# Three of a block's turns by DMA instead of TensorE, and another list of the round, in a four-layer graph network on one Trainium2 core

## The reference

```python
# 0: GCN over the normalized adjacency, two linear layers (256-512-256), each with a batchnorm over all tokens
x = _layernorm(x + _L0_gnn_ref(x, adj, ...))
# 1: Chebyshev mix, linear, layernorm, relu, plus x (x1); masked attention with 4 heads, plus x1, layernorm (x2);
#    MLP 256-512-256 with gelu, plus x2, layernorm
x = _layernorm(x + _L1_gnn_ref(x, adj, adj, ...))
# 2: two graph convolutions, then for p = 1..4 an LSTM over windows of p tokens whose last state replaces a token
x = _layernorm(x + _L2_gnn_ref(x, adj, ...))
# 3: Wh = x @ W; attention from s1 + s2, leaky relu, mask, softmax; attention @ Wh
x = _layernorm(x + _L3_gnn_ref(x, adj, ...))
```

## Time and profile before

| | us |
|---|---|
| median of 3 runs | 2158.94 |
| lowest, highest | 2158.62, 2160.29 |
| the profiled execution, its own time | 2162.29 |
| its span, first to last instruction | 2160.5 |
| TensorE busy in the span | 2017.1 |
| VectorE busy | 1749.8 |
| ScalarE busy | 1451.9 |

### The profile page before, as it was taken

One profiled execution on the slowest core, in us unless ns is written; L12 is line 12 of the kernel. 1 busy time (PEld: TensorE's weight loads), 2 busy tenths in 40 slices (PEclk: granted clock), 3 DMA queues, 4 the chain that ended last, 5 costly groups with the idle time before them and its releaser, 6 DMA issues. The chain is left out here.

```text
span 2160.5 us, 86772 instructions
## 1 busy us (share of the span) xinstructions
PE 2017.1 (93%) x37609; PEld 1780.4 (82%) x37609; DVE 1749.8 (81%) x4987; ACT 1451.9 (67%) x4411; POOL 187.0 (9%) x259
## 2 busy tenths in 40 slices
PE   6979769999999999999999999999999999999986
PEld 3434358989898989889898989898989998899985
DVE  6779767888888888888888888888888888888865
ACT  5657336767776777667676776676767766676775
POOL 2000000000001000100010000101010001000000
PEclk9989789999999999999999999999999999999998
DMA  7847300000100001000100010000000010000000
GB/s 277 289 173 267 107 11 12 13 12 3 41 3 22 3 3 42 12 12 3 42 13 12 3 41 13 12 3 28 16 22 3 3 42 12 12 3 12 3 12 12
DMA packets 36825, 87.85 MB, mean 41 GB/s; under 512 B 2416, under 2 KB 26992, under 8 KB 32752
## 3 DMA queue, kind: packets, MB, share of 16 engines
q1 hardware_dynamic: 36464, 82.56, 11.0%
HBM read 52.15 MB, written 30.41 MB: 38 GB/s over the span
## 5 line engine op out<-in xcount | busy, mean ns | idle before, releaser
L1443 ACT ACTIVATE pool_mem<-ps,lstm_b 128x64 f32<-128x64 f32 (+2 forms) x2496 | 603.9, 354 | 191.8 <-PE ps L252 186.4
L250 PE MATMUL ps<-hl_a,w_hi 128*128 128x64 f16 (+2 forms) x3776 | 545.6, 215 | 31.9 <-DVE hl_a L623 16.0
L251 PE MATMUL ps<-hl_a,w_hi 128*128 128x64 f16 (+2 forms) x3776 | 544.3, 215 | 0.0
L252 PE MATMUL ps<-hl_a,w_lo 128*128 128x64 f16 (+2 forms) x3776 | 543.8, 215 | 0.0
L250 PEld LDWEIGHTS ps<-hl_a,w_hi 128*128 128x128 f16 x3776 | 350.5, 98 | 64.0 <-DVE hl_a L623 17.1
L251 PEld LDWEIGHTS ps<-hl_a,w_hi 128*128 128x128 f16 x3776 | 350.2, 98 | 24.4 <-issue 3.0
L252 PEld LDWEIGHTS ps<-hl_a,w_lo 128*128 128x128 f16 x3776 | 350.2, 98 | 24.4 <-issue 3.0
L250 PE MATMUL ps<-hl_b,w_hi 128*128 128x84 f16 (+2 forms) x2112 | 366.3, 228 | 2.5 <-ACT pool_mem L1443 1.7
L251 PE MATMUL ps<-hl_b,w_hi 128*128 128x84 f16 (+2 forms) x2112 | 366.0, 228 | 0.0
L252 PE MATMUL ps<-hl_b,w_lo 128*128 128x84 f16 (+2 forms) x2112 | 364.3, 228 | 0.0
L250 PE MATMUL ps<-pool_mem,w_hi 128*128 128x64 f16 (+2 forms) x3072 | 352.4, 200 | 2.2 <-DVE pool_mem L1716 2.0
(11 more groups left out here) (244 smaller groups left out, 4402.1 us busy)
## 6 DMA issues: line engine op xcount, KB each, us to landing
xa<-in_x SPq DMA_DIRECT2D x32, 512.0 KB, 5.5
h_scratch<-pool_mem SPq DMA_DIRECT2D x14, 1024.0 KB, 4.3
pool_mem<-h_scratch SPq DMA_DIRECT2D x14, 1024.0 KB, 6.8
pool_mem<-in_wpack SPq DMA_DIRECT2D x16, 704.0 KB, 4.3
out<-xb SPq DMA_DIRECT2D x16, 512.0 KB, 3.4
o_scratch<-act_in SPq DMA_DIRECT2D x14, 512.0 KB, 3.2
act_in<-o_scratch SPq DMA_DIRECT2D x14, 512.0 KB, 5.4
row<-in_rows SPq DMA_DIRECT2D x1, 1408.0 KB, 11.4
```

Of the source, the lines that this page charges most:

```text
L250: nc.tensor.matmul(o, l[0], r[0], start=first, stop=False, skip_group_check=True)
L251: nc.tensor.matmul(o, l[0], r[1], start=False, stop=False, skip_group_check=True)
L252: return nc.tensor.matmul(o, l[1], r[0], start=False, stop=last, skip_group_check=True)
L1443: op = nc.scalar.activation(gates[s][h][:, g, m * w:(m + 1) * w], gate_place(s, h, g, m, w), ACT.Tanh, bias=lstm_b[:, bias:bias + 1], scal ...
```

## The change

The three turns leave TensorE. ScalarE and VectorE split x1, x2 or xc while it still lies by token, into `by_token_hl` (in the place of the LSTM's state, which is free then): ScalarE's `turn_high` writes hi from the buffer x1, VectorE's `turn_low` writes x1 minus hi. SP then issues two transposing DMAs per half, each from 128 tokens x (2 parts x 256 features) to 4 blocks of 128 features x 128 tokens in hl_b, and v, mlp_up and gat wait until both have landed. In diff form, cut:

```diff
+            TURNS = ["x1", "x2", "xc"]
+            turn_hi = Signal("turn_hi", " ".join(TURNS))
+            turn_lo = Signal("turn_lo", " ".join(TURNS))
+            turned = Signal("turned", " ".join(TURNS))
...
+                def landed(self, s, n, h, which):
+
+                    sem, count = self.at(s, n, h, which)
+                    return sem, count * HALF * 16
...
+                def turn(s, n, h, which):
+                    sp.wait_ge(*turn_lo.at(s, n, h, which))
+                    for b in range(HALF):
+                        a = h * HTOK + b * P
+                        sp.dma_start(hl_b[s][:, :, :, a:a + P].rearrange("p c k n -> p (c k) n"),
+                                     by_token_hl[s][h][:, b, :, :].rearrange("p c d -> p (c d)"), transpose=True)\
+                            .then_inc(turned.of(s, h), 16)
...
-                def turn(s, n, h, src, which):
-
-                    bank = FEAT_BANK[which][h]
-                    for f in range(KT):
-                        for b in range(HALF):
-                            mm = nc.tensor.transpose(fea(s, bank)[:, f, b * P:(b + 1) * P],
-                                                     src[s][:, h * HALF + b, f * P:(f + 1) * P], ident[:, :])
-                    mm.then_inc(feat_ps.of(s, h), 1)
...
                 def value(s, n, h):
-                    pe.wait_ge(*feat_lo.at(s, n, h, "x1"))
+                    pe.wait_ge(*turned.landed(s, n, h, "x1"))
...
+                    nc.scalar.copy(by_token_hl[s][h][:, :, 0, :], x1[s][:, blocks(h), :]).then_inc(turn_hi.of(s, h), 1)
...
+                def turn_low(s, n, h, which):
+                    dve.wait_ge(*turn_hi.at(s, n, h, which))
+                    hi, lo = (by_token_hl[s][h][:, :, c, :] for c in range(2))
+                    nc.vector.tensor_tensor(lo, x1[s][:, blocks(h), :], hi, ALU.subtract).then_inc(turn_lo.of(s, h), 1)
```

```diff
+                    if (base, s, n) not in reached:
+                        reached.add((base, s, n))
+                    elif base == "turn_x1" and n > 1:
+                        store_tile(s, n - 1)
+                    elif base == "turn_x2" and n < ROUNDS:
+                        load_next_o(s, n)
+                    elif base == "hid3" and n < ROUNDS:
+                        load_next_x(s, n)
```

The list ROUND has the same steps in another order (two of its lines, the first of each):

```diff
-1:xa_bias.0 1:turn_x1.0 0:inp3.0 0+norm_y 1:cheb.1 0:hid3.1 0:cell3.0 0:pack3.1 1:conv.1 0:hid3.0 1:norm_g1.1
+1:cheb.1 0:pack3.1 0:cell3.0 1:conv.1 0:hid3.0 1:norm_g1.1 1:v.0 0:pack3.0 1:q.0 1:k.0 0:inp4.1 1:xa_bias.1
```

More of the change, by code:

```diff
@@ new lines @@
+1:turn_x1.1 0:inp4.0 0:cell4.1 1:scores.0 0:cell4.0 0:hid4.0 0:hid4.1 1:exps.0 0:inp5.0 1:v.1 1:q.1 1:k.1 1:scores.1
+1:exps.1 0:inp5.1 0:cell5.1 0:cell5.0 0:hid5.1 1:turn_probs.1 0:hid5.0 0:inp6.1 1:attend.1 0:cell6.1 0:hid6.1
+1:turn_probs.0 1:attn_out.1 0:pack4.1 1:norm_g2.1 0:inp6.0 0:cell6.0 1:turn_x2.1 1:attend.0 0:hid6.0 0:inp7.1
+0:cell7.1 0:pack4.0 1:attn_out.0 1:norm_g2.0 0:hid7.1 0:inp7.0 0:cell7.0 1:mlp_up.1 1:gelu_split.1 1:turn_x2.0
+0:hid7.0 0:inp8.1 0:cell8.1 1:mlp_down.1 0:inp8.0 0:hid8.1 1:mlp_up.0 1:norm_g3.1 1:gelu_split.0 1:norm_l1.1 0:inp9.1
@@ new lines @@
+0:cell9.1 0:hid9.1 1:mlp_down.0 1:mix0.1 1:norm_g3.0 0:inp10.1 0:cell10.1 0:cell8.0 0:hid10.1 1:gcn0.1 1:norm_l1.0
+0:hid8.0 0+norm_y 0:inp9.0 0:turn_state.1 1:mix1.1 0:cell9.0 0:norm_l2.1 0:hid9.0 0:turn_xc.1 1:mix0.0 0:inp10.0
+1:gcn1.1 0:cell10.0 0:hid10.0 1:gcn0.0 0:gat.1 0:turn_state.0 0:gat_exps.1 0:norm_l2.0 1:inp0.1 1:cell0.1 1:mix1.0
+0:turn_xc.0 0:turn_att.1 1:hid0.1 1:inp1.1 0:gat_mix.1 1:cell1.1 1:gcn1.0 0:norm_l3.1 0:gat.0 1:hid1.1 1:inp0.0
+1:cell0.0 0+turn_y.1 1:hid0.0 1:inp1.0 0:gat_exps.0 0:turn_att.0 0+norm_l0.1 0:gat_mix.0 1:cell1.0 0+cheb.1 1:inp2.1
@@ new lines @@
+1:hid1.0 1:cell2.1 0:norm_l3.0 0+conv.1 1:hid2.1 0+turn_y.0 1:inp2.0 0+norm_g1.1 0+norm_l0.0 1:cell2.0 1:inp3.1
+1:cell3.1 0+cheb.0 0+xa_bias.1 0+turn_x1.1 1:hid2.0 1:inp3.0 0+conv.0 0+norm_g1.0 1+norm_y 1:cell3.0 0+v.1 0+xa_bias.0
+0+turn_x1.0 1:hid3.0 0+q.1 0+k.1 1:pack3.0 0+scores.1 1:inp4.0 1:cell4.0 0+exps.1 1:hid4.0 0+v.0 1:hid3.1 0+q.0 0+k.0
+0+turn_probs.1 0+scores.0 0+attend.1 1:pack3.1 0+exps.0 1:inp5.0 1:cell5.0 0+attn_out.1 1:hid5.0 0+turn_probs.0
+0+norm_g2.1 1:inp4.1 1:cell4.1 0+attend.0 1:inp6.0 0+turn_x2.1 1:cell6.0 1:hid6.0 1:hid4.1 0+attn_out.0 1:inp5.1
@@ L104 @@
+1:gat_exps.0 0+gcn1.0 1:turn_att.0 1:norm_l2.1 1:gat_mix.0 1:turn_xc.1 0+inp0.0 0+cell0.0 1:norm_l3.0 0+hid0.0
+0+inp0.1 0+cell0.1 1+turn_y.0 0+inp1.0 0+hid0.1 0+inp1.1 0+cell1.0 0+cell1.1 1+norm_l0.0 0+hid1.1 1:gat.1 1+cheb.0
+0+hid1.0 1:gat_exps.1 0+inp2.1 0+cell2.1 1+conv.0 1:turn_att.1 1:gat_mix.1 0+inp2.0 0+hid2.1 0+cell2.0 1:norm_l3.1
+1+norm_g1.0 0+inp3.1 1+turn_y.1 0+cell3.1 1+norm_l0.1 0+hid2.0 0+hid3.1 1+xa_bias.0 1+turn_x1.0 0+inp3.0
 """.split()
@@ L1037, in build @@
             state = of_half(2048, 2560, "p (k n) -> p k n", k=KT)
+            by_token_hl = [[m[:, 2048:2560].bitcast(F16).rearrange("p (b c d) -> p b c d", b=HALF, c=2) for m in halves]
+                           for halves in part]
             state_hl = FEAT_DST["h1"]
```

81 lines of the change are left out of this document (46 added, 35 removed).

## The result

The changed kernel takes **2255.64 us** (median of 4 runs, 2253.08 to 2259.28) against 2159.25 for the kernel before in the same comparison: a ratio of 1.0447, 95% interval [1.0429, 1.0465]. It is slower by 96 us. The forecast was 2141 us with a range of 2117 to 2222, so sign and range were both missed.

What follows compares the result with a forecast made beforehand. TensorE, 93% busy, was taken to bound the seven middle rounds, engine-to-engine delay the two ends. 2162.3 - 12.6 (rounds) - 9.6 (loads) - 14 (waits) + 17.6 (ends) = 2143.7, against the median 2141 us; range 2117 to 2222.

Steps and rivals of the forecast that it cites:

- D = 2.7 us: Time for a turn's pair of transposing DMAs before v, mlp_up or gat, taken between 16 KB and 512 KB rows.
- the forecast's own walk: Model pricing step orders by TensorE issue and each half's own chain; 1812 us for a measured 1905, only differences used.
- the 9.6 and the 14: Two forecast gains in us: 9.6 from loads of act_in issued earlier, 14 from waits the walk does not model.
- The slow pair: Rival: D is 3.4 us or more, waits before v, mlp_up and gat; 2187 us at D = 4.0; chance 0.25.
- Block by block: Rival: each transposing DMA handles its four blocks in turn, D 6.3 us, about 2318 us; chance 0.1.
- TensorE -42.2: 384 transposes in 96 turns leave TensorE at 0.44 us a turn: 42.2 us less, 5.3 a round.
- ScalarE and VectorE, nothing: Copy and subtraction of a turn take about as long from SBUF as from PSUM; no cost expected.
- Rounds: Seven middle third-pass rounds: 5.3 of transposes less 3.5 of new list gaps gains 1.8 us each, -12.6; rounds at 224 to 228.
- Loads: SP loads act_in over 70 us ahead of norm_y, ending ScalarE's wait in six rounds: 6 x 1.6 = -9.6 us.
- Scores behind k: Second halves of both streams: scores stands right behind k with nothing between, a new 0.95 us gap each.
- waits beyond the walk: Middle-round waits the walk misses, largest before the GAT attention's transposes: 2 us a round removed, 14 in all.
- The two ends: Opening and closing together grow 17.6 us, 8 of it from turns in uncovered chains; 8 to 22 possible.

Runs made afterwards that it cites:

- one_of_two: The change with only the first of each pair's two transposing DMAs, TensorE waiting for it alone (half the tokens not moved): 2169.2 us, ratio 1.0032.
- old_list: The change with the step order of the kernel before; turns still by transposing DMAs, SP's plain DMAs placed by the list: 2466.5 us, ratio 1.1408.
- sp_by_list: The kernel before, own step order and TensorE transposes kept; only SP's plain third-pass loads and stores placed by the list: 2157.0 us, ratio 0.9973.
- single_right: The change with one transposing DMA of 256 KB per turn instead of two, rounded values laid in block order, features correct: 2191.8 us, ratio 1.015.
- plain_copies: The change with plain copies in place of the transposing DMAs, same bytes and places, features not turned: 2196.3 us, ratio 1.0156.
- none_old: The change without any of the 192 transfers and with the step order of the kernel before (does not compute the reference): 2147.2 us, ratio 0.9937.
- none_new: The change without any of the 192 transfers, its new step order kept (does not compute the reference): 2147.3 us, ratio 0.9934.
- list_alone: The kernel before with only the change's new step order; turns stay on TensorE, SP's loop stays: 2276.1 us, ratio 1.0533.
- list_and_sp: The kernel before with the change's new step order and SP's plain DMAs placed by it; turns stay on TensorE: 2276.4 us, ratio 1.0526.

## Why the prediction was wrong

**D = 2.7 us is the step that failed.** It was taken half way between the landings of a 16 KB and a 512 KB DMA; measured, 3.82 in the median and 4.27 on the mean. The landing alone was priced well: one transposing DMA lands in 2.5. What was left out of the central value is that a pair goes through SP one after the other, and that each takes SP 1.26 us. The upper bound had this very sum (3.4 + 3 x 0.40 = 4.6, "three times as long to issue"), and it was the true one: 2.5 + 1.26. With D near the forecast's (one_of_two, 2.48 in the median, 2.82 on the mean) the time is 2169, so of the miss of 115 us 86 go with D on the chip, and what is left is 22 us in the rounds (-14 for -36) and 6 in the two ends. By the forecast's own walk the measured D was worth less: +69 us under the new list (in what was expected of old_list), which less the 9.6 and the 14 is 2205. The other 50 us are a second failure, of the price that the walk puts on D.

**The slow pair** was the rival that came true, and decided as it said, with waits of 1 us and more before v, mlp_up and gat. Its price did not hold: at D = 4.0 it gave +28 us and at 4.6 +63, where the change lost 96 at a mean of 4.27. The walk let a turn's copy start as soon as its own norm was ready. It had room of 7.4 to 16.5 us where counting from the turn's place in the list leaves 4.1 to 8.5. The chain that it had at 1.4 + 2.7 = 4.1 us behind the norm was, by the means, 0.91 until the copy starts, 1.78 until the split has ended and 4.27 for the pair, 7.0 together; in old_list 3.08, 1.99 and 4.04, 9.1 together. old_list shows this part most plainly: 319 us for transfers of the same length in a list with shorter distances, a part of them at the lower clock. It was said that the walk "knows TensorE and a half's own chain, not that ScalarE and VectorE serve four halves in turn", and then only differences were used; but the difference sought was made by just that.

**Block by block** is out: four blocks land in 2.5 us and eight in 3.1, 0.15 us for each further block. The Trainium skill's "VectorE: DVE Perf Modes", The three transpose paths, has 1309 ns for one 128x128 block by DMA; worked out from that, an estimate, a pair would have been near 10.5 us, and the runs contradict it when several blocks share a DMA. The advice of that page's Rules for kernel authors, to transpose on TensorE where PSUM will do, holds here all the same: sp_by_list, with the turns on TensorE, takes 2157 us and single_right, the best with DMAs, 2192. "Advanced Engine Details and Errata" in the Trainium skill, X-Bar Transpose (TRN2), has transposing DMAs as fast as regular ones: for the landing this case agrees (2.5 against 2.3 us in plain_copies), for SP's issue it does not (1.26 against 0.61).

**TensorE -42.2**: the transposes went (37,609 matmuls became 37,225, the difference being the 384), and 96 x 0.44 us of issue with them. What that is worth was assumed to be nearly all of it in the middle rounds. With the old list and no transfer at all it was 10 us (2157 to 2147). In the seven rounds 37 us of issue went and 7 us of time; TensorE's waits for ScalarE and VectorE grew from 47.4 us in sp_by_list to 69.0 in none_old, so most of the rest came back there.

**ScalarE and VectorE, nothing**: right as a duration (0.62 and 0.68 us), wrong as a place in the queue (the 0.91 and 1.78 above).

**Rounds**: 5.3 - 3.5 = 1.8 and 2 us of further waits each, with 1.6 for the loads in six, made -36 for the seven; none_new has -27.7 with D = 0, one_of_two -14.0. The change has +55.4. **Loads**: -9.6 forecast, 4.5 to 7 gained in sp_by_list, nothing between list_alone and list_and_sp; no wait for act_in is left in the change either. **Scores behind k**: forecast 0.95, measured 0.94 in each round for both streams. **GAT's transposes**: their wait went from 9.9 us to

```profile
PE ps L1353 <- ACT pool_mem L1502: 4.3, 5, 0.9
```

(same stretch of time), so part of the "waits beyond the walk" was really removed, and swamped. It is the list's doing: from 600 to 2000 us this wait is 5.2 us in list_alone and 9.9 in none_old. **The two ends**: +17.6 forecast, +40.4 measured; without transfers +15.5, so the list's part was sized well and the transfers' not. The granted clock fell there too, from 0.83 to 0.79 in the opening and from 0.97 to 0.92 in the closing: at the lower level, 1.2 GHz, stood 35 us of the opening before and 53 in the change, 10 and 30 us of the closing. none_new, whose two ends are shorter by 11 and 14 us, has 0.82 and 0.94, with 40 and 23 us.

## What to carry to other kernels

Before a step leaves the busiest engine for a DMA, add up the whole new chain with its issue: two DMAs in one queue land one issue later than one, and here no row of the kernel before had that issue, only the changed kernel's trace. Then count the cover (the work that TensorE has to do meanwhile) from the place where the in-order engines that feed the transfer reach it, not from where its data could be ready; where four streams of work share those queues, placing it earlier blocks the others and placing it later uncovers the transfer. An engine that is 93% busy is no promise: 42 us off it brought 10 when two others behind it were 81 and 67% busy.

## What the runs showed of the hardware

- A transposing DMA from SBUF to SBUF occupies SP's queue for about 1.25 us whether it has 2, 4 or 8 blocks of 128x128 in 2-byte values (medians 1.246, 1.262, 1.237); a plain copy of 128 KB in pieces took 0.61. From issue to landing it takes 2.4, 2.5 and 3.1 us. One large DMA beats two small ones by 0.7 us of D.
- The change's 192 transposing DMAs (25 MB) go over the DMA engines in small pieces: 141,272 packets in place of 36,825, and of the 104,447 more all are under 512 B (106,864 in place of 2,416). plain_copies, which moves the same bytes without turning them, has 138,200 packets. The DMA engines' share in a round went from 3 to 5% to 12 to 13%, and nothing in these runs shows another transfer hurt by it.
- D has two humps. 54 of the 96 pairs in the change take 3.72 to 3.99 us, the other 42 take 4.06 to 5.78. In the packet records each of the 42 overlaps a packet of the queues named "instruction"; of the 54, more than 30 overlap none and some 20 overlap one without harm. That is an observation of one trace: no experiment took these packets away, so that they cause the 0.45 us by which the mean lies above the median is not shown. Plain copies have the second hump too (about a third of the 96).
